# First expert group tile by tile, gather indices written from PSUM, and layer 0's tokens kept in the scatter banks

## The chip, the cores and the metric

One core of one Trainium2 chip. The metric is device time in microseconds (us) of one execution; a run's figure is a median over executions.

## The reference

Four layers work on x, 4 sequences of 256 tokens with 256 channels (1024 tokens in all). Each layer l first makes a gated input and then adds the result of a feed-forward part:

```
c = sigmoid(x) * ratio_l          # ratio_l: a two-way decayed scan over time of exp(k) and exp(k)*v (numerator / denominator)
x = x + ffn_l(c)
```

- Layer 0: every sequence picks its 32 best tokens by a router (128 picked tokens); they go through attention (16 heads) and an MLP of width 1024; the result, times a gate per token, is added at the picked tokens. x also gets c itself.
- Layer 1: mixture of 64 experts. sigmoid(c @ gate) are the scores; 4 of 8 groups of experts and then 6 experts are picked per token; each expert has 48 places (slots) and runs silu(g) * u, width 96, then a down product; the slots' results, times weights, are added to their tokens. A shared expert of width 96 is added for every token.
- Layer 2: 8 experts given as low-rank corrections of one shared MLP of width 704. Layer 3: a dense gated MLP of width 1024.

## The kernel before, in words

Each engine has one instruction list, written out by hand; engines wait for each other by semaphores. Channels lie on the partitions: `xT`, `cT` and so on are 128 partitions x 2 halves (`ct`) x 1024 tokens, and a product over all tokens is cut into two chunks (`ch`) of 512. So the eight PSUM banks of 512 columns hold, for instance, the four (`ct`, `ch`) pieces of a full result in banks 0 to 3. The scans of the ratios of later layers (`forth`, L742: forward scans; `back_again`, L753: backward scans; `den`, L759; `num_own`, L764; `num`, L769; `newton`, L776 and L778; `quotient`, L783) are spread by hand between VectorE's other work.

**End of layer 0.** TensorE sums the output projection `wo` (L1478), then runs filler products that nothing reads (`idle`, L1355), turns the normalized rows `xn` (L1425), runs the gate and up products (L1490) into banks 0 to 3 and the down product (L1495) into bank 5. VectorE adds `ao` and multiplies by the gate (L963, L964) to make `dl`; TensorE scatters `dl` by the one-hot matrix into banks 0 to 3 (L1500). VectorE had added `cT` to `xT` before (L959), and now adds each bank to `xT` (L970); ScalarE takes the sigmoid of `xT` (L477); VectorE multiplies by `ratio` (L792) to make the new `cT`, then runs four scans (L742).

**Routing of layer 1.** TensorE makes the logits (L1509), turns tokens to rows (L1362) and scores to rows (L1515); from there VectorE finds groups, experts and slots (L977 to L1032). Three 4-byte products (L1549) turn the slot numbers so that VectorE can write the token of each slot, first as numbers (`tokf`, L1035) and then cast to whole numbers (`toki`, L1037). The tokens' rows lie in DRAM (`token_rows`: 256 channels and 64 weights), written by SyncE's queue: rows at L316, weights `w1` at L318. GpSimd waits for these writes, clears two pads (L380) and issues indirect gathers (L391), three of 128 slots for each of 8 groups of 8 experts; the gathers of group g+2 wait until group g's hidden rows are turned. SyncE loads the weights of the next but one group (L307, L308) when a group's down product is done.

**The loop over 8 groups.** For each: `rows_in` turns the gathered rows (TensorE L1566, copies by ScalarE L589), `gate_up` (L1603), silu (L596), product (L1083), `turn_hidden` (L1612, copied at L604), `down` (L1629), scaled copies (L638, L639), the rest part (L1069), the one-hot matrices (L1063), and 24 scatter products into banks 0 to 3 (L1574), which run one group late. `slot_weights` is L1054 and L1055. VectorE's scans for layers 2 and 3 fill the rest. In group 0 the order of VectorE is: wait for all three gathers, `back_again(2, 0, 0)`, `forth(2, 0, 1)`, the products of the group, `slot_weights(0)`, `back_again(2, 0, 1)`, two `den`, one-hots, rests. On TensorE filler products stand before and after `rows_in(0)`, and two of the four products of the shared expert's down part (L1555) stand before it, two just before `down(0)`.

Of the kernel before, what the change touches and what calls it, by code (L numbers as in the profile page):

```python
# [24 lines left out]
P = 128  # L25
# [23 lines left out]
GE = 8  # L49
# [44 lines left out]
def build(nc, I, out):  # L94
    ctx = ExitStack()
    with ctx:
# [28 lines left out]
        rows1 = sb("rows1", [P, RRING, 2, C], F32R)  # L125
        bank = [ctx.enter_context(nc.psum_tensor(f"bank{i}", [P, CHUNK], F32)) for i in range(6)]
# [67 lines left out]
        spreadv = at(o + N, GE, CAP)  # L194
# [66 lines left out]

        def tail2(it):

            return it % H2T == H2T - 1
# [8 lines left out]
        def _(sp):  # L273
# [24 lines left out]
            sp.wait_ge(S("x1_ready"), 4)  # L298
# [52 lines left out]
        def _(pool):  # L351
# [23 lines left out]
            pool.wait_ge(S("x1_ready"), 4)  # L375
# [9 lines left out]
            for t in range(ST):  # L385
                if t % GT == 0 and t >= 2 * GT:
                    pool.wait_ge(S("h1_turned"), 2 * (t // GT - 1))
                if t >= XRING:
                    pool.wait_ge(S("xgT_done"), (t - XRING) // GT + 1)
                    pool.wait_ge(S("wslot_ready"), (t - XRING) // GT + 1)  # L390
                g.indirect_dma_start(xg[:, t % XRING, :], None, scratch[:, :],  # L391
                                     bass.IndirectOffsetOnAxis(ap=toki[:, t:t + 1].bitcast(U32), axis=0)
                                     ).then_inc(S(f"gather{t // GT % 4}"), 16)
# [22 lines left out]
        def _(act):  # L416
# [54 lines left out]
            def gate(l):  # L471
                for ct in range(CT):
                    if l == 0:
                        act.wait_ge(S("x_in"), 16)
                    else:
                        act.wait_ge(S(f"x{l}_ready"), 2 * ct + 2)
                    s.activation(cT[:, ct, :], xT[:, ct, :], ACT.Sigmoid).then_inc(S("sig_ready"), 1)  # L477

# [31 lines left out]
            gate(0)  # L510
# [50 lines left out]
            for j in range(2):  # L561
                act.wait_ge(S("gate0_done"), j + 1)
                s.activation(su0[:, 4 * j:4 * j + 4, :], bank[j][:].rearrange("p (a c) -> p a c", a=4), ACT.Silu).then_inc(S("silu0"), 1)

            gate(1)
# [18 lines left out]
            def rows_in(g):  # L584
                for ct in range(CT):
                    act.wait_ge(S("xgT_done"), g + 1)
# [19 lines left out]

            euk(2)
            rows_in(0)
# [98 lines left out]
        def _(dve):  # L707
# [80 lines left out]
            def cond(l):  # L788
                dve.wait_ge(S("ratio_ready"), l)
                for ct in range(CT):  # L790
                    dve.wait_ge(S("sig_ready"), 2 * l + ct + 1)
                    v.tensor_tensor(cT[:, ct, :], cT[:, ct, :], ratio[l % 2][:, ct, :], ALU.mult).then_inc(S("c_ready"), 1)  # L792
# [144 lines left out]
            num(1, 0)  # L937
            num(1, 1)
# [3 lines left out]
            v.tensor_copy(ao, bank[4][:, 0:C])  # L942
# [9 lines left out]
            for j in range(2):  # L952
# [3 lines left out]
                                bank[2 + j][:].rearrange("p (a c) -> p a c", a=4), ALU.mult).then_inc(S("hm0_ready"), 1)  # L956
                if j == 0:
                    for ct in range(CT):
# [988 lines left out]
```

## Time and profile before

| | |
|---|---|
| median of 3 runs | 456.92 us (455.61 to 457.77) |
| the profiled execution, its own time | 456.5 us |
| its span, first to last instruction | 454.7 us |
| granted TensorE clock, mean | 0.968 |
| busy: TensorE / VectorE / ScalarE / GpSimd | 88% / 79% / 47% / 24% |

Times in the profile count from the span's start. A busy share says nothing by itself of what sets the end; for that one follows which wait ends last in each stretch. A 4-byte float product appears as two instructions, one of type fp32r as one.

### The profile page before, as it was taken

The numbers are of one execution on the slowest core, as the hardware profiler recorded it, in microseconds if no ns is written. First come the engines' busy times: TensorE is split into PE (matmuls) and PEld (weight loads), VectorE is DVE, ScalarE is ACT, GpSimd is POOL, SyncE is SP. The second block draws the span as 40 slices with busy tenths as digits, with TensorE's granted clock in tenths as the row PEclk, the third lists the DMA queues.
The fourth block names the chain that finished last, engine by engine and source line by source line (L and its number), as shares of the span: only waits on it lengthen the run. The fifth ranks groups of instructions, "written<-read, shape, count | busy, mean of one in ns | idle before, by whom it ended". The sixth has DMA issues, their size and how long they took to land.

```text
span 454.7 us, 5110 instructions
## 1 busy us (share of the span) xinstructions
PE 400.9 (88%) x1680; PEld 216.3 (48%) x1680; DVE 360.4 (79%) x663; ACT 215.9 (47%) x398; POOL 108.5 (24%) x76
## 2 busy tenths in 40 slices
PE   0988999989988597998999999999999999998673
PEld 0433454677834255675677773444444344433220
DVE  4999969885989679897997879617986966449995
ACT  2864655563236645656774683521111141157780
POOL 1000004200000233343220000047684844540000
PEclk9999899989999599999999999999999999999897
DMA  7930000550039328775677530350000000000011
GB/s 278 396 155 1 2 0 0 210 196 0 1 129 322 104 64 222 209 237 159 214 232 241 215 116 1 138 233 0 1 0 0 0 0 1 1 0 0 1 48 46
DMA packets 12251, 47.45 MB, mean 104 GB/s; under 512 B 2897, under 2 KB 5434, under 8 KB 9794
## 3 DMA queue, kind: packets, MB, share of 16 engines
q1 hardware_dynamic: 11074, 43.20, 27.0%
q0 software_dynamic: 1152, 3.93, 3.8%
q8 instruction: 14, 0.23, 0.2%
q14 instruction: 11, 0.09, 0.1%
HBM read 44.76 MB, written 2.37 MB: 104 GB/s over the span
## 4 chain that ended last, share of the span: by engine, by line
PE 45%; DVE 29%; issue 14%; POOL 5%; DMA 4%; ACT 2%; POOLq 0%; DVEq 0%; SPq 0%
PE bank L1710 7%; PE bank L1697 6%; POOL arena L391 5%; PE bank L1574 4%; PE bank L1742 3%; PE bank L1739 3%; PE bank L1446 3%; DMA arena<-token_rows,arena 2%; PE bank L1355 2%; PE bank L1665 2%; PE bank L1490 2%; PE bank L1478 2%; PE bank L1629 1%; DMA vecs<-in_vecs 1%; DVE ekT L1319 1%
## 5 line engine op out<-in xcount | busy, mean ns | idle before, releaser
L676 ACT ACTIVATE early<-bank 128x512 f32<-128x512 f32 (+1 forms) x24 | 14.3, 597 | 86.0 <-PE bank L1710 76.6
L1574 PE MATMUL bank<-onehot,rows 128*128 128x512 f32 x192 | 52.4, 413 | 0.0
L1244 DVE TENSOR_TENSOR early<-early,bank 128x512 f32<-128x512 f32 (+1 forms) x24 | 16.4, 685 | 37.8 <-ACT early L676 34.3
L391 POOL DMA_INDIRECT arena<-token_rows,arena x24 | 30.6, 1275 | 54.4 <-PE bank L1612 48.5
L1710 PE MATMUL bank<-arena 128*128 128x512 f32 (+1 forms) x96 | 42.2, 600 | 0.1
L1574 PEld LDWEIGHTS bank<-onehot,rows 128*128 128x128 f32 x192 | 34.7, 193 | 10.3 <-issue 3.5
L1697 PE MATMUL bank<-cT,arena 128*128 128x512 f32 x80 | 37.9, 596 | 0.0
L402 POOL TENSOR_TENSOR early<-early,arena 128x512 f32<-128x512 f32 (+1 forms) x12 | 20.1, 1672 | 62.4 <-DMA arena<-pair_weights 55.6
L408 POOL TENSOR_TENSOR early<-early,arena 128x512 f32<-128x512 f32 x10 | 22.3, 2232 | 29.6 <-DVE early L1244 29.6
L1063 DVE TENSOR_SCALAR onehot<-const,arena 128x1024 fp32r<-128x1024 f32 x24 | 18.0, 754 | 10.7 <-PE bank L1574 10.3
L1710 PEld LDWEIGHTS bank<-arena 128*128 128x128 f32 (+1 forms) x96 | 15.7, 181 | 22.6 <-issue 21.2
L1697 PEld LDWEIGHTS bank<-cT,arena 128*128 128x128 f32 x80 | 14.9, 190 | 18.1 <-issue 18.1
L371 POOL TENSOR_TENSOR arena<-arena 128x512 f32<-128x512 f32 x6 | 8.0, 1335 | 63.9 <-DVE arena L908 63.9
L1742 PE MATMUL bank<-early,arena 128*128 128x512 f32 x48 | 22.8, 596 | 0.0
L1603 PE MATMUL bank<-arena 128*64 128x192 f32 x256 | 22.5, 329 | 0.1
L1629 PE MATMUL bank<-arena 96*64 96x256 f32 x192 | 22.5, 383 | 0.0
L1355 PE MATMUL bank<-const 128*128 128x512 f32 x42 | 22.0, 649 | 0.0
L1739 PE MATMUL bank<-early,arena 128*128 128x512 f32 (+1 forms) x48 | 21.3, 605 | 0.8 <-POOL early L406 0.8
L1762 PE MATMUL bank<-wkv_a,arena 128*128 128x512 bf16 x64 | 17.2, 409 | 5.1 <-DVE wkv_a L1217 2.6
L412 POOL TENSOR_TENSOR early<-early 128x512 f32<-128x512 f32 x10 | 21.0, 2100 | 1.6 <-PE bank L1742 0.9
L1603 PEld LDWEIGHTS bank<-arena 128*64 128x64 f32 x256 | 18.1, 137 | 5.0 <-issue 3.0
L1629 PEld LDWEIGHTS bank<-arena 96*64 96x64 f32 x192 | 13.1, 137 | 9.4 <-issue 3.6
(367 smaller groups left out, 858.9 us busy)
## 6 DMA issues: line engine op xcount, KB each, us to landing
arena<-in_w_gateup SPq DMA_DIRECT2D x16, 768.0 KB
arena<-in_w_down SPq DMA_DIRECT2D x8, 768.0 KB
arena<-in_wq SPq DMA_DIRECT2D x1, 2048.0 KB
arena<-in_wo SPq DMA_DIRECT2D x1, 2048.0 KB, 7.7
const<-in_const SPq DMA_DIRECT2D x1, 1688.0 KB, 10.7
arena<-in_w_upgate SPq DMA_DIRECT2D x1, 1408.0 KB, 5.8
kT<-in_kT SPq DMA_DIRECT2D x2, 512.0 KB, 4.9
xT<-in_xT SPq DMA_DIRECT2D x1, 1024.0 KB, 7.9
```

The lines of the kernel that those rows point to most:

```text
L391: g.indirect_dma_start(xg[:, t % XRING, :], None, scratch[:, :], bass.IndirectOffsetOnAxis(ap=toki[:, t:t + 1].bitcast(U32), axis=0)).then ...
L402: g.tensor_tensor(c1[r1], t1[r1], c1b[r1, cc], ALU.mult).then_inc(S("ch_ready"), 1)
L408: g.tensor_tensor(c2[r2], t2[r2], c2b[r2, cc], ALU.mult).then_inc(S("ch_ready"), 1)
L412: g.tensor_tensor(mix[r1], c1[r1], c2[r1], ALU.add).then_inc(S("ch_ready"), 1)
L1355: mm(bank[bk][:], ident, iota[:, 0:CHUNK], start=True, stop=True)
L1574: return mm(bank[2 * ct + ch][:], rows1[:, i % RRING, part, ct * P:(ct + 1) * P], onehot1[:, t, ch * CHUNK:(ch + 1) * CHUNK], start=False, ...
L1603: last = mm(bank[4 + p // 2][HALF * h:HALF * (h + 1), (p % 2) * 2 * F1:(p % 2 + 1) * 2 * F1], xgT[g % 2][:, ct, e * CAP:e * CAP + HALF], r ...
L1629: last = mm(bank[6 + t // 2][HALF * h:HALF * (h + 1), (t % 2) * C:(t % 2 + 1) * C], h1[:, RUN4 * j + lo:RUN4 * j + lo + HALF], r["d"][:, 4 ...
L1697: mm(bank[2 * (it % 2) + z][:], wug2[:, ct, z * 5 * P + f * P:z * 5 * P + (f + 1) * P], cT[:, ct, ch * CHUNK:(ch + 1) * CHUNK], start=(ct ...
L1710: last = mm(dst, (bup, bga)[z][:, f * P:f * P + fw], ((zu1, zg1), (zud, zgd))[k][z][:, ch * CHUNK:(ch + 1) * CHUNK], start=False, stop=Tru ...
L1739: mm(bank[6 + k][:], adn[rows2(it, k), f, :], cc_[rows2(it, k)], start=(f == 0), stop=(f == H2T - 1))
L1742: last = mm(bank[4 + ct][:], wdn2[:, f, ct * P:(ct + 1) * P], c1 if tail2(it) else mix, start=(f == 0), stop=False)
```

## The change

Two stretches are edited: from the `wo` product to the routing of layer 1, and from the slot numbers to the end of group 0.

```
# layer 0
VectorE:  xT += cT moves from between the two hidden products to before num(1, 1)   (L959)
          ao = wo result * gate (was a plain copy); dl = down * gate + ao in one instruction (was two)
          the four additions of the banks to xT are gone
TensorE:  idle(7, 5)  ->  keep_tokens(0), keep_tokens(1);   idle(7, 1)  ->  keep_tokens(2)
          gate and up products to banks 4 to 7, down product to bank 4, then keep_tokens(3)
          scatter products start=True -> start=False;  idle(6, 2) gone
+            def keep_tokens(i):
+                ct, ch = divmod(i, 2)
+                pe.wait_ge(S("c0_ready"), B + ct + 1)
+                mm(bank[i][:], ident, xT[:, ct, ch * CHUNK:(ch + 1) * CHUNK], start=True, stop=False)
ScalarE:
+            def gate1():
+                for i in range(4):
+                    ct, ch = divmod(i, 2)
+                    act.wait_ge(S("scatter0_done"), i + 1)
+                    s.activation(cT[:, ct, ch * CHUNK:(ch + 1) * CHUNK], bank[i][:], ACT.Sigmoid).then_inc(S("sig_ready"), 1)
+            def rows1_kept():        # four copies of banks 0 to 3 to xT, ahead of the scores' sigmoid
+                    s.copy(xT[:, ct, ch * CHUNK:(ch + 1) * CHUNK], bank[i][:]).then_inc(S("x1_ready"), 1)
VectorE:  the product with ratio in four pieces of 512 (was two of 1024); logits wait for each piece
SyncE and GpSimd no longer wait for x1_ready before the expert weights and the clears
TensorE waits for x1_ready only before it turns tokens to rows

# layer 1, slots
+        groups1 = sb("groups1", [P, GE], F32R)
+        spreadv = sb("spread1", [P, GE, CAP], F32R)          # L1549 becomes three one-pass products
+            v.tensor_copy(groups1[:], ofgroup)
+            v.tensor_scalar(toki.bitcast(U32).rearrange("p (g t) -> p t g", t=GT), slots,
+                            float(N), float(N), ALU.add, ALU.min).then_inc(S("toki_ready"), 1)
+            v.tensor_scalar(tokf.rearrange("p (g t) -> p t g", t=GT), slots, float(N), float(N), ALU.add, ALU.min).then_inc(S("toki_ready"), 1)

# layer 1, group 0
+        FIRST_GATHER = "gather0", "gather3", "gather2"       # one semaphore for each of the three gathers
+            def first_rows(t):                               # TensorE; ScalarE has one copy for each to match
+                pe.wait_ge(S(FIRST_GATHER[t]), 16)
+                for ct in range(CT):
+                    last = tr(bank[(6, 7, 0)[t]][:, ct * P:(ct + 1) * P], xg[:, t, ct * P:(ct + 1) * P], ident)
+                last.then_inc(S("xgT_done"), 1)
-            idle(6, 3)
-            rows_in(0)
-            idle(5, 1)
+            first_rows(0)
+            first_rows(1)
+            gate_up(0, (0,))
+            first_rows(2)
+            gate_up(0, (1, 2, 3))
+            shared_down(0, 0)
+            shared_down(0, 1)
ScalarE:  a Silu on one column after euk(2), before the first copies
VectorE:  forth(2, 0, 1) moves from right behind back_again(2, 0, 0) to behind slot_weights(0)
```

## Rows read from the trace of the kernel before

**Rows 1.** The page, busy time by engine.
```profile
PE 400.9 (88%) x1680; PEld 216.3 (48%) x1680; DVE 360.4 (79%) x663; ACT 215.9 (47%) x398; POOL 108.5 (24%) x76
```
**Rows 2.** Windows: stretch, length, busy us (instructions) by engine, clock, DMA share, GB/s.
```profile
162.00:175.00 13.00, 12.58 (x106) 8.81 (x106) 12.69 (x23) 9.26 (x23) 5.75 (x4) 1.00 0.32 74
187.00:199.00 12.00, 12.00 (x89) 8.78 (x88) 10.44 (x17) 7.35 (x15) 3.53 (x2) 1.00 0.84 225
```
**Rows 3.** Timeline, before the gate and up products: start, us, engine, line [idle before].
```profile
109.77 4.46 PE L1355 MATMUL bank<-const 128*128 128x512 f32 x10
109.97 0.42 DVE L940 TENSOR_TENSOR arena<-bank,arena 128x256 f32<-128x256 f32 x1 [3.08 <-PE bank L1478]
...
111.42 0.35 DVE L945 TENSOR_SCALAR arena<-arena 128x256 f32<-128x256 f32 x1
114.06 0.38 PE L1425 MATMUL bank<-const,arena 128*128 128x128 f32 x2
...
115.14 3.06 PE L1490 MATMUL bank<-arena 128*128 128x128 f32 x25
```
**Rows 4.** Timeline, from the hidden products of layer 0 to its scatter.
```profile
120.38 2.35 DVE L959 TENSOR_TENSOR xT<-xT,cT 128x1024 f32<-128x1024 f32 x2
...
122.39 3.62 PE L1495 MATMUL bank<-arena 128*128 128x256 f32 x16
...
126.11 0.42 DVE L963 TENSOR_TENSOR arena<-bank,arena 128x256 f32<-128x256 f32 x1
...
126.98 3.70 PE L1500 MATMUL bank<-arena 128*128 128x512 f32 x8 [0.97 <-DVE arena L964]
...
128.15 0.69 DVE L970 TENSOR_TENSOR xT<-xT,bank 128x512 f32<-128x512 f32 x1 [1.22 <-PE bank L1500]
```
**Rows 5.** The chain of waits, into the routing: start, us, what.
```profile
131.32 2.43 DVE cT L792 x2
...
136.38 0.70 DVE arena L977
```
**Rows 6.** Timeline, ScalarE's copies of four banks.
```profile
138.62 2.01 ACT L571 COPY arena<-bank 128x512 f32<-128x512 f32 x4
```
**Rows 7.** Timeline, from the slot numbers to group 0.
```profile
153.50 1.45 PE L1549 MATMUL bank<-const,arena 128*128 128x8 f32 x6 [5.68 <-DVE arena L1032]
...
154.78 0.20 POOL L380 MEMSET arena<- 128x32 f32 x2 [22.25 <-DMA token_rows<-arena]
...
155.21 0.18 DVE L1037 CAST arena<-arena 128x24 uint32<-128x24 f32 x1
...
161.67 2.68 DVE L753 TENSOR_TENSOR_SCAN wkv_c<-dec,ends,wkv_c 128x256 f32<-128x256 f32 x4 [5.09 <-DMA arena<-token_rows,arena]
...
164.21 2.82 PE L1603 MATMUL bank<-arena 128*64 128x192 f32 x32
...
166.91 0.35 DVE L1083 TENSOR_TENSOR arena<-arena,bank 128x192 f32<-128x192 f32 x1
```
**Rows 8.** The chain of waits, the first gathers.
```profile
155.68 1.16 POOL arena L391
...
158.40 3.24 DMA arena<-token_rows,arena
```
**Rows 9.** Timeline, TensorE's first work of group 1 after its wait.
```profile
178.86 0.42 PE L1612 MATMUL bank<-const,arena 128*96 128x128 f32 x2 [2.52 <-DVE arena L1083]
```
**Rows 10.** Windows with the clock at half (columns as in Rows 2).
```profile
150.00:159.00 9.00, 5.50 (x11) 2.95 (x12) 4.89 (x14) 5.49 (x11) 2.91 (x5) 0.50 0.25 55
180.00:183.00 3.00, 3.00 (x10) 2.06 (x8) 3.00 (x5) 2.20 (x4) 1.12 (x1) 0.50 1.04 264
```
**Rows 11.** Timeline, a gather that landed late (group 4).
```profile
198.59 0.80 SPq L307 DMA_DIRECT2D arena<-in_w_gateup  x2
...
199.41 0.95 POOL L391 DMA_INDIRECT arena<-token_rows,arena  x1 [0.30 <-issue]
...
208.15 0.87 PE L1566 MATMUL bank<-const,arena 128*128 128x128 f32 x6 [2.12 <-DMA arena<-token_rows,arena]
```

More of the change, by code:

```diff
@@ L509, in _ @@
             euk(0)
-            gate(0)
+            gate0()
             for j in range(4):
@@ L562, in _ @@
                 act.wait_ge(S("gate0_done"), j + 1)
-                s.activation(su0[:, 4 * j:4 * j + 4, :], bank[j][:].rearrange("p (a c) -> p a c", a=4), ACT.Silu).then_inc(S("silu0"), 1)
-            gate(1)
+                s.activation(su0[:, 4 * j:4 * j + 4, :], bank[(4, 6)[j]][:].rearrange("p (a c) -> p a c", a=4), ACT.Silu).then_inc(S("silu0"), 1)
+            gate1()
+            rows1_kept()
             act.wait_ge(S("logit1_done"), 1)
@@ L605, in hidden_copy @@
                        bank[4 + j][0:F1, 0:4 * HALF].rearrange("f (e c) -> f e c", c=HALF)[:, :, 0:CAP]).then_inc(S("h1_ready"), 1)
+            def first_rows(t):
+                act.wait_ge(S("xgT_done"), t + 1)
+                s.copy(xgT[0][:, :, t * P:(t + 1) * P],
+                       bank[(6, 7, 0)[t]][:, 0:C].rearrange("p (a c) -> p a c", a=CT)).then_inc(S("xgT_ready"), 1)
             euk(2)
-            rows_in(0)
+            s.activation(ws1[:, 0:1], ws1[:, 0:1], ACT.Silu)
+            for t in range(GT):
+                first_rows(t)
             for g in range(NG):
@@ L1046, in _, with all_gathered @@
             shared_product(1)
[L1047 removed]
+            def all_gathered(g):
+                if g:
+                    dve.wait_ge(S(f"gather{g % 4}"), gathered(g))
+                else:
+                    for name in FIRST_GATHER:
+                        dve.wait_ge(S(name), 16)
+            all_gathered(0)
             back_again(2, 0, 0)
[L1049 removed]
             def slot_weights(g):
[L1052 removed]
+                all_gathered(g)
                 i = g * GT
@@ L1494, in _ @@
                 pe.wait_ge(S("hm0_ready"), f // 4 + 1)
-                last = mm(bank[5][:, 0:C], hm0[:, f, :], wd0[:, f, :], start=(f == 0), stop=(f == F0T - 1))
+                last = mm(bank[4][:, 0:C], hm0[:, f, :], wd0[:, f, :], start=(f == 0), stop=(f == F0T - 1))
             last.then_inc(S("down0_done"), 1)
+            keep_tokens(3)
             pe.wait_ge(S("dl_ready"), 1)
@@ L1548, in _ @@
             for t in range(GT):
-                last = mm(bank[4][:, t * NG:(t + 1) * NG], spreadv.rearrange("e g c -> e (g c)")[:, t * P:(t + 1) * P], ofgroup,
+                last = mm(bank[4][:, t * NG:(t + 1) * NG], spreadv[:].rearrange("e g c -> e (g c)")[:, t * P:(t + 1) * P], groups1[:],
                           start=True, stop=True)
```

112 lines of the change are left out of this document (50 added, 62 removed).

## The prediction

> **What bounds the kernel now.** I read the page first, for the shares: TensorE is busy 88% of the span and VectorE 79% [rows 1], so neither share alone says what sets the end, and the stretches have to be read one by one. Then the windows: in the stretch of group 0 VectorE is busy 12.69 of 13.00 us, and from group 2 on TensorE is busy 12.00 of 12.00 [rows 2]. The chain of waits and the timeline fill in the rest, and in them I look only at the two stretches that the change edits, because all that stands before and after is untouched and can only be shifted. The reader should see four facts. (1) Ahead of the gate and up products TensorE is not waiting for data: `xn` is written at 111.42 + 0.35 = 111.77, but TensorE turns it only at 114.06, because ten filler instructions hold it for 4.46 us from 109.77 [rows 3]. (2) From the scatter to the routing the path is a relay: scatter, addition, sigmoid, product with the ratio, four scans, and routing at 136.38 [rows 4, 5]. (3) From there to the slot numbers VectorE runs alone and TensorE idles, for 5.68 us before the slot products [rows 7]. (4) VectorE waits 5.09 us for the three first gathers, and from their landing at 158.40 + 3.24 = 161.64 it works almost without a gap until TensorE, which has been idle for 2.52 us, is let go at 178.86 [rows 7, 8, 9]. After that TensorE is the bound. So a gain counts if it brings the landing of the gathers forward, or shortens VectorE's work from there to 178.86.
>
> **The change part by part.** Times are those of the trace before, and each shift is counted against it.
>
> *Fillers ahead of the MLP.* Ten filler instructions cost 4.46 us, 0.446 each. Two `keep_tokens` are four such instructions, 1.78 us: from 109.77 to 111.55. Then `xn` (111.77) is late next, and the turning starts at about 111.82 instead of 114.06: gain 2.24 us [rows 3]. `keep_tokens(2)` is as long as the filler that it replaces. The additions of `cT` to `xT` (2.35 us, [rows 4]) move into VectorE's wait of 3.08 us for the `wo` product [rows 3]; they are hidden with 0.7 us to spare, and without that cover the whole 2.35 would stand ahead of `xn`. `ao` with a scalar costs what the copy did, and lies beside ScalarE's square root.
>
> *The MLP and its end.* Gate and up, and the down product (3.62 us, [rows 4]), only change banks. VectorE loses the additions between the two hidden products, but these ended at 120.38 + 2.35 = 122.73 and the up products only just before the down products began at 122.39, so the second hidden product was at most 0.3 us late, and the down products had their first half to do meanwhile: 0. `dl` by one instruction of about 0.42 instead of two (126.11 to 126.98, 0.87) saves 0.45 us on VectorE. But `keep_tokens(3)`, two instructions of 0.446, stands on TensorE between down product and scatter: it ends 0.89 us after the down product, while `dl` is there 0.09 + 0.43 = 0.52 after it. So the scatter starts 0.89 us behind the down product instead of 0.96 (126.98 against 126.02, the product's end). Gain 0.07; sum 2.3.
>
> *From scatter to routing.* Before: the first bank is read at 128.15, the last when the scatter ends, 126.98 + 3.70 = 130.7, and the last `cT` stands at 131.32 + 2.43 = 133.75, 3.05 us after the last bank [rows 4, 5]. After: sigmoid of 512 columns from PSUM, which I take at ScalarE's copy of the same shape (four in 2.01, so 0.50 in a row, [rows 6]) plus 0.1 for one alone, then a product of 512 columns on VectorE at 0.69 as L970 has it, and a hand-over: 0.6 + 0.05 + 0.7 = 1.35 after the last bank. Gain 1.7. Bounds: 1.2 if all pieces queue, 2.0 if less. The path then forks. VectorE goes on with four scans. TensorE must end the logits, ScalarE must end `rows1_kept`, four copies, 2.01 us [rows 6], before the scores' sigmoid, which is queued behind them. The copies end 0.6 + 2.0 = 2.6 us after the last bank, the logits about 1.35 + 0.9 for two product instructions + 0.2 of hand-overs = 2.45: the copies decide by 0.15, and take back 0.1 to 0.3 of the gain. Behind the waiting sigmoid stand the scaling for a scan and the row copies, all with time to spare. Gain so far 2.3 + 1.7 - 0.2 = 3.8, and the routing starts at 136.38 - 3.8 = 132.6.
>
> *Slots.* VectorE's search in between is untouched; the small copy to `groups1` adds at most what the small cast L1037 takes, 0.18 [rows 7], in a place where VectorE waits for TensorE's counts; I take 0. Six product instructions in 1.45 us become three: 0.24 each, 0.72 [rows 7]; gain 0.7 (no less than 0.4, no more than 0.9). `toki` straight from PSUM saves the cast, 0.18 and its hand-over: 0.2 [rows 7]. That would be 0.9, but GpSimd also waits for the write of `w1`, and this write only moves with the routing (3.8). It releases the clears at 154.78 and they end at 154.98, against a first gather at 155.68 [rows 7, 8]. The write and the clears are late next: 154.98 - 3.8 + 0.3 for the issue = 151.4, so the first gather gains 4.3 us, 0.5 from this part and not 0.9. Expert weights start with the scatter's end (124.7 + 3.7 = 128.4) and no longer wait for the last addition (130.7 + 0.7): 3 us earlier, out of the way of the `w1` write as before.
>
> *Group 0.* The last gather lands at 161.64 - 4.3 = 157.3. TensorE before needs 164.21 + 2.82 - 161.64 = 5.4 us from there to the end of gate and up [rows 7, 8]; by tiles, with one quarter done, it needs two turnings (0.4), then three quarters of 2.82, 2.5 us in all. That is 2.9 us more for TensorE, but VectorE does not use it: its list from landing to TensorE's release holds the same work in another order, `back_again` 2.68 first, after which both silu are ready within 0.1 us (157.3 + 2.5 + some 0.4 for the silu, against 157.3 + 2.7 + 0.35 for the first product). Before, VectorE had idled only a few tenths there (its product stands at 166.91, right behind the scans). So I count 0 for this edit (at most 0.2), and TensorE, 7 us early with `down(0)`, waits for VectorE in group 1 for longer than 2.52 us. The two `shared_down` in between lie in that slack. `tokf` after `toki` costs 0.2 in VectorE's wait for the gathers.
>
> Sum: 2.3 + 1.7 - 0.2 + 0.5 + 0 = 4.3 us. The profiled execution took 456.5, so 452.2; the median of the runs shown is 0.4 above that execution, so 452.6.
>
> **The clock.** TensorE runs at half clock (0.50) from 150 to 159 and again from 180 to 183 [rows 10], each time after an idle stretch, of 5.68 and 2.52 us [rows 7, 9]. The change leaves the first idle stretch as it is, removes the fillers that came before and after `rows_in(0)`, and lengthens the second. If the clock is not back when the last gather lands, gate and up of three quarters take 2.1 us longer, VectorE's second product is late by about that, and a longer low clock in group 1 costs some tenths: a loss of 2.1. The Trainium skill, "TensorE: Matmul & The Clock Gate", section "Why this matters for your kernels", speaks for this rival: it advises not to leave gaps between bursts of products, and the change takes out products that filled such a gap. By that rule the time is 454.7, by the rows' sum 452.6; the trace agrees with the rule in that both half-clock stretches follow an idle one.
>
> **Rivals.**
> - *Half clock at group 0.* 452.6 + 2.1 = 454.7. For it: rows 10. Against it: TensorE still has two filler instructions and four `shared_down` ones, some 5 us at half clock, before the first gather lands. Chance 0.20.
> - *The gathers start with the index list.* If the `w1` write lands sooner, or VectorE finds a tenth here and there, the gain is 4.7 to 5.5: 451.7. Chance 0.10.
> - *No change.* The gain at the front is real but is taken back later: VectorE's and TensorE's loop is aligned with loads, and a longer low-clock stretch in group 1 (the present one, 180 to 183, cost half of 3 us) or `rows1_kept` ahead of the scores' sigmoid eats it. 456.5. Chance 0.13.
> - *Slower: gathers behind the weights.* In group 4 the last gather was issued at 199.41, after the group's weights at 198.59, and TensorE waited 2.12 us for it [rows 11]. It decides as soon as a group's last gather is issued after the weights of the same phase. If the shifted order makes four more groups wait so, 4 x 2.12 = 8.5 against 4.3: 452.6 + 8.5 = 461.1. Against it: the order inside groups 1 to 7 is unchanged, and both queues shift together. Only group 2's gathers move against their weights. Chance 0.07.
>
> **How the numbers follow.** My forecast has 0.50, the rivals 0.20, 0.10, 0.13 and 0.07. A measurement of this kernel tells 0.5% (2.3 us) from no change, so faster means below 454.6. Faster: 0.50 + 0.10 + half of the clock's rival, 0.10, and a little of the fourth, 0.02 = 0.72. Same: 0.21. Slower: 0.07. The range reaches from 5.9 us of gain (all upper bounds: 2.3 + 2.0 + 0.9 + 0.2, and half a us of the clock) to the clock's rival with 0.7 more: 451.0 to 455.4; it holds the first three cases, 0.80.
>
> **What would show it.** TensorE's turning of `xn` right after `xn` is written, near 111.8; scatter start near 124.7; the four sigmoids 0.86 apart; the first routing instruction (L977 before) near 132.6; three slot products of 0.2 to 0.3 us; first gather near 151.4, released by the `w1` write and not by `toki`; last landing near 157.3; end of gate and up 2.5 us later; TensorE let go in group 1 near 174.5 after a wait for VectorE. The prediction is wrong if VectorE has gaps in group 0, if the clock is low after 157, or if the groups from 2 on take longer than before.

## The result, and the profile after

The changed kernel takes 452.85 us (median of 5, 451.23 to 454.70) against 455.90 for the kernel before on the same chip: a ratio of 0.9927 [0.9898, 0.9957], 3.1 us less. In 12 more executions, beside 35 of the kernel before at 456.01, it took 452.53 (450.18 to 454.53), ratio 0.9930 [0.9898, 0.9961], 3.5 us less. (Executions more than 1.5% above the fastest of their kernel are left out of the ratios, not of the medians.) The forecast was 452.6, 4.3 us less than the median of 456.92 that stood for the kernel before. The kernel before now has a median 1.0 us lower, and the fall is about 1 us smaller than forecast; the two cancel. That the median stands so near 452.6 is luck, and the fall of 3.1 to 3.5 us is what the working has to answer for.

The execution whose profile is read here is the longest of the first five, 454.7. That is the very time of the clock's rival, and the profile shows that the clock had a part in it. A second profile of the same kernel, from an execution of 453.1, is read beside it. Places in traces are best compared from VectorE's `x1` on (109.97 in [rows 3]), the addition behind the `wo` product, because the place of `x1` itself differs by almost 4 us between the executions (108.60 to 112.44). It is 109.49 after, and 111.10 in the second profile. "From `x1`" below means this difference. From the loop's end to the last instruction it takes 181.2 to 181.6 us in all 14 profiles, so `x1` and the loop's end account for the whole time.

The mark has one weakness. TensorE's list up to the `wo` product is untouched, but VectorE's two additions of `cT` to `xT` now stand ahead of `x1`. In the two profiles of the change `x1` starts 0.20 us behind the end of the `wo` product, as before. In four of the experiments it does not; the table below says which.

The page after: span, TensorE's, VectorE's and ScalarE's busy time, and the clock in 40 slices.

```profile
span 452.8 us, 5081 instructions
...
PE 399.1 (88%) x1661; PEld 215.3 (48%) x1661; DVE 357.8 (79%) x661; ACT 217.8 (48%) x406; POOL 106.8 (24%) x76
...
PEclk9999899989999587999999999999999999999798
```

Against [rows 1] the sums hardly move: 1.8 us less on TensorE, 2.6 on VectorE. They say nothing of where 3 us went, so the stretches are read one by one. First the timeline after, from the additions of `x1` to the routing (start, us, engine, line, tile, idle time before and its releaser).

```profile
109.29 1.88 PE L1508 MATMUL bank<-xT,const 128*128 128x512 f32 x4
109.49 0.42 DVE L965 TENSOR_TENSOR arena<-bank,arena 128x256 f32<-128x256 f32 x1 [0.81 <-PE bank L1502]
...
111.35 0.44 PE L1449 MATMUL bank<-const,arena 128*128 128x128 f32 x2 [0.18 <-DVE arena L971]
...
112.49 7.41 PE L1521 MATMUL bank<-arena 128*128 128x128 f32 x64
...
124.06 3.60 PE L1532 MATMUL bank<-arena 128*128 128x512 f32 x8
...
127.69 0.60 ACT L485 ACTIVATE cT<-bank 128x512 f32<-128x512 f32 x1 [0.26 <-PE bank L1532]
...
128.18 2.05 ACT L490 COPY xT<-bank 128x512 f32<-128x512 f32 x4
128.32 0.69 DVE L815 TENSOR_TENSOR cT<-cT,ratio 128x512 f32<-128x512 f32 x1 [0.17 <-ACT cT L485]
...
130.18 0.60 ACT L581 ACTIVATE arena<-bank 128x512 f32<-128x512 f32 x1
...
131.62 0.69 DVE L992 TENSOR_TENSOR arena<-bank,early 128x512 f32<-128x512 f32 x1
```

The reader is to see three things. The turning of `xn` (L1449) now follows VectorE by 0.18 us; four `keep_tokens` instructions take the place of ten fillers. The scatter starts 14.57 us from `x1`, before 17.01: a gain of 2.44. The last `cT` stands at 129.01, 19.52 from `x1` against 23.78, so the tail behind the scatter gave another 1.82. The routing starts 22.13 from `x1` against 26.41 [rows 5]: 4.28 earlier, and 22.12 in the second profile.

Now the timeline after, from the slot numbers to the end of group 0, which answers to [rows 7] and [rows 8].

```profile
148.74 0.80 PE L1580 MATMUL bank<-groups,spread 128*128 128x8 f32 x3 [5.68 <-DVE spread L1048]
...
149.57 0.19 DVE L1052 TENSOR_SCALAR arena<-bank 128x24 uint32<-128x24 f32 x1 [0.90 <-PE bank L1580]
...
150.01 0.20 POOL L385 MEMSET arena<- 128x32 f32 x2 [21.31 <-DMA token_rows<-arena]
...
150.84 1.16 POOL L396 DMA_INDIRECT arena<-token_rows,arena  x1 [0.63 <-issue]
...
156.33 1.55 PE L1642 MATMUL bank<-arena 128*64 128x192 f32 x8
...
157.18 2.68 DVE L774 TENSOR_TENSOR_SCAN wkv_c<-dec,ends,wkv_c 128x256 f32<-128x256 f32 x4 [6.14 <-DMA arena<-token_rows,arena]
...
158.43 3.98 PE L1642 MATMUL bank<-arena 128*64 128x192 f32 x24
...
160.39 0.35 DVE L1106 TENSOR_TENSOR arena<-arena,bank 128x192 f32<-128x192 f32 x1 [0.53 <-ACT arena L610]
...
162.83 0.35 DVE L1106 TENSOR_TENSOR arena<-arena,bank 128x192 f32<-128x192 f32 x1 [2.08 <-ACT arena L610]
...
176.79 0.66 PE L1651 MATMUL bank<-const,arena 128*96 128x128 f32 x2 [2.81 <-DVE arena L1106]
```

The first gather stands 41.35 from `x1` against 45.71: 4.36 earlier. VectorE takes up its scans at the landing, 47.69 against 51.70: 4.0 earlier. But then it waits 0.53 and 2.08 us for the two silu, because three quarters of gate and up take 3.98 us. The same stretch in the second profile of this kernel:

```profile
158.78 2.68 DVE L774 TENSOR_TENSOR_SCAN wkv_c<-dec,ends,wkv_c 128x256 f32<-128x256 f32 x4 [6.15 <-DMA arena<-token_rows,arena]
...
159.13 2.17 PE L1642 MATMUL bank<-arena 128*64 128x192 f32 x24
...
161.37 0.69 DVE L1106 TENSOR_TENSOR arena<-arena,bank 128x192 f32<-128x192 f32 x2
```

Here the three quarters take 2.17 us and both products stand in a row with no wait. The windows tell what differs (length, busy us and instructions by engine, granted clock, DMA share, GB/s), first in the profile after, then in the second.

```profile
154.00:159.00 5.00, 4.56 (x20) 2.25 (x20) 1.82 (x3) 1.12 (x3) 3.77 (x4) 0.50 0.54 126
159.00:163.00 4.00, 4.00 (x26) 2.60 (x23) 1.39 (x4) 0.66 (x2) 0.00 (x0) 0.61 0.16 44
```

```profile
154.00:159.00 5.00, 4.13 (x17) 1.65 (x16) 0.22 (x1) 0.74 (x2) 3.78 (x5) 0.76 0.49 122
159.00:163.00 4.00, 4.00 (x30) 2.44 (x29) 3.92 (x9) 1.03 (x3) 1.29 (x1) 1.00 0.36 93
```

The clock is at half (0.50) from 145.1 to 162.2 in the one and from 146.1 to 156.4 in the other, with the same instructions in the same order. One execution gets 2.4 GHz back before the products need it, the other only as they end.

The gain can be followed through the whole program in one table: us from `x1` to VectorE's scans at the landing, to the first one-hot of group 0, to TensorE's gate and up of group 2, and to the first product of layer 2 behind the last scatter (L1665 before, L1705 after), where the loop is over.

| | landing | one-hot, group 0 | gate and up, group 2 | loop over |
|---|---|---|---|---|
| before | 51.70 | 63.35 | 79.88 | 163.31 |
| after, first profile | 47.69 | 61.90 | 79.59 | 161.96 |
| after, second profile | 47.68 | 59.17 | 76.18 | 158.68 |

In the second profile the 4.0 us of the landing are 3.7 at group 2 and 4.6 at the end. In the first, 2.6 go in group 0 and another 1.2 in group 1, so that 0.3 are left at group 2 and 1.3 at the end. From group 2 on both profiles are about 1 us shorter than the one of before (82.4 and 82.5 against 83.4), in groups that the change doesn't touch; whether that comes with the change isn't shown. The first profile's 454.7 is 1.8 us below the 456.5 of before: 1.3 from this table, and 0.5 from the untouched part ahead of `x1`. So the gain at the front is in both executions, and most of what comes through is decided between 157 and 180 us.

### The profile page after: what moved, and what is told of

Same layout as the page of the kernel before. It is cut to its first block, busy times and chain, and to the rows that moved or that the text cites. A ratio compares the mean times of both kernels' runs of the same rounds, so it can differ in the third digit from the quotient of the medians.

```text
span 452.8 us, 5081 instructions
## 1 busy us (share of the span) xinstructions
PE 399.1 (88%) x1661; PEld 215.3 (48%) x1661; DVE 357.8 (79%) x661; ACT 217.8 (48%) x406; POOL 106.8 (24%) x76
## 4 chain that ended last, share of the span: by engine, by line
PE 46%; DVE 27%; issue 15%; POOL 4%; DMA 4%; ACT 3%; POOLq 0%; DVEq 0%; SPq 0%
PE bank L1750 7%; PE bank L1737 6%; POOL arena L396 4%; PE bank L1603 4%; PE bank L1782 3%; PE bank L1779 3%; PE bank L1470 3%; DMA arena<-token_rows,arena 2%; PE bank L1642 2%; PE bank L1705 2%; PE bank L1521 2%; PE bank L1502 2%; PE bank L1668 1%; DVE ekT L1343 1%; DVE ekT L1346 1%
## 5 line engine op out<-in xcount | busy, mean ns | idle before, releaser
L396 POOL DMA_INDIRECT arena<-token_rows,arena x24 | 29.2, 1216 | 59.4 <-PE bank L1651 53.5
L1642 PE MATMUL bank<-arena 128*64 128x192 f32 x256 | 25.2, 353 | 0.0
L774 DVE TENSOR_TENSOR_SCAN wkv_c<-dec,ends,wkv_c 128x256 f32<-128x256 f32 x16 | 10.7, 731 | 6.2 <-DMA arena<-token_rows,arena 6.1
```

What stands on the lines that cost most here:

```text
L1642: last = mm(bank[4 + p // 2][HALF * h:HALF * (h + 1), (p % 2) * 2 * F1:(p % 2 + 1) * 2 * F1], xgT[g % 2][:, ct, e * CAP:e * CAP + HALF], r ...
```

## The experiments

Each kernel ran 12 times beside the kernel before on the same chip (the last two 6 times), with one profile. Three chips were used: one for again, layer0_only, group0_only and fed_search, one for scans_first to early_pads, one for the last four. Nothing of the computation is left out in any. Ratios are to the kernel before on the same chip, with their 95% intervals, and kernels of different chips are compared by them.

One table for their profiles, in the columns above, with the stretch of half clock ahead of or in group 0 (us in that profile, and its end from `x1`; before it ends at 159.4 or 49.4, after at 162.2 or 52.7, in the second profile at 156.4 or 45.3):

| | median us, ratio | landing | one-hot | group 2 | loop over | half clock, end from `x1` |
|---|---|---|---|---|---|---|
| layer0_only | 455.62, 0.9964 [0.9930, 0.9999] | 48.27 | 60.92 | 78.33 | 162.21 | 144.8 to 158.5, 48.4 |
| group0_only | 456.85, 1.0021 [0.9992, 1.0049] | 51.76 | 63.37 | 79.62 | 163.31 | 149.8 to 160.1, 48.6 |
| fed_search | 456.27, 0.9992 [0.9957, 1.0027] | 47.48 | 61.69 | 78.84 | 163.33 | 152.3 to 162.6, 52.1 |
| scans_first | 453.88, 0.9938 [0.9893, 0.9983] | 47.46 | 58.86 | 76.30 | 158.96 | 146.9 to 157.1, 45.2 |
| fed_all | 453.38, 0.9947 [0.9912, 0.9982] | 47.47 | 58.96 | 75.22 | 161.31 | 142.2 to 145.6, 37.0 |
| fillers_back | 456.99, 1.0013 [0.9980, 1.0047] | 47.47 | 61.65 | 78.93 | 162.90 | 147.4 to 157.7, 45.5 |
| early_pads | 452.40, 0.9939 [0.9902, 0.9975] | 47.44 | 58.93 | 75.88 | 159.08 | 144.5 to 154.7, 44.9 |
| layer0_no_fill | 455.94, 0.9988 [0.9950, 1.0026] | 47.40 | 60.42 | 76.63 | 159.05 | 146.2 to 163.2, 52.7 |
| before_no_fill | 457.17, 1.0004 [0.9970, 1.0039] | 51.68 | 65.50 | 80.12 | 165.01 | 150.8 to 161.1, 48.6 |
| gathers_first | 449.12, 0.9850 [0.9797, 0.9902] | 47.46 | 59.08 | 75.90 | 155.49 | 146.9 to 157.2, 45.3 |
| both_mends | 450.31, 0.9885 [0.9836, 0.9935] | 47.48 | 59.02 | 75.84 | 155.43 | 146.3 to 156.5, 45.3 |

In layer0_only, fed_all, early_pads and layer0_no_fill `x1` starts 0.93 or 0.94 us behind the end of the `wo` product (TensorE's next instruction marks it), and not 0.20 as in all others. VectorE has no wait there, as in early_pads:

```profile
108.67 1.22 DVE L790 TENSOR_TENSOR wkv_a<-wkv_a,wkv_d 128x1024 f32<-128x1024 f32 x1
108.87 1.88 PE L1508 MATMUL bank<-xT,const 128*128 128x512 f32 x4
...
109.81 0.42 DVE L965 TENSOR_TENSOR arena<-bank,arena 128x256 f32<-128x256 f32 x1
```

So 0.7 us of the front's gain are lost ahead of `x1` in these four, where the columns don't show them: 0.7 belongs on each of their entries when they are compared with other rows. They are also just the four profiles without a stretch of half clock between 97 and 103 us; the other ten have one of 3.4 us there (98.0 to 101.4 before). Without it the `wo` product ends sooner against VectorE's list: 5.85 us behind the start of `num_own` in early_pads (103.02 to 108.87), 7.49 in the first profile of the change (101.80 to 109.29). Then the moved additions are no longer covered.

**again**: the changed kernel, unedited, for a second profile and a better median.

> The changed kernel itself, once more. Its profiled execution took 454.7 us, but others took 451.23 and 451.6. Theory A (the clock): executions differ in when TensorE's clock comes back after the search for slots. In the profiled one it was back at 162, after the last gather's landing at 157.2, and VectorE waited 0.53 + 2.08 us for gate and up; an execution in which it is back before the landing should take 451 to 452, with no such waits, and one in which it is not 453 to 455. Theory B (the order): the waits come from the new order alone, since VectorE no longer has four scans to run while gate and up are made; then a profile with an earlier clock still shows about 2 us of waits.

Its profile is read above. It is theory A's picture, the clock back at 156.4, ahead of the landing, and no wait of VectorE for gate and up. It took 453.1 and not 451 to 452, with an `x1` 1.6 us later than in the first profile.

**layer0_only and group0_only**: the change cut in two. The first has layer 0's edits, with group 0 and the slots as before; the second the reverse.

```
layer0_only = before + keep_tokens, gate1, rows1_kept, ao and dl, the four pieces
group0_only = before + one-pass slot products, toki from PSUM, first_rows, order of group 0
```

> Only the edits to layer 0 (tokens kept in the scatter banks, sigmoid from the banks, fused dl, logits by pieces); slots and group 0 as before. By the prediction's sum 2.3 + 1.7 - 0.2 = 3.8 us faster than the kernel before, so 452.1 against 455.9. If the sum of the whole is right but the two halves are not what I think, this would gain under 2.5 us. The fillers of group 0 are in place here, so by theory A its executions should spread less than those of the whole change.

> Only the edits to slots and group 0 (one-pass slot products, indices from PSUM, rows by tiles, scans behind slot_weights); layer 0 as before. By the prediction's sum 0.5 us faster (the first gather is held by the write of the weights w1), so 455.4. Theory A: in executions whose clock is late it loses up to 2.1 and is 1.6 slower than before, so 455.4 to 457.5. Theory B: always about 1.5 slower.

By their ratios layer 0's edits alone bring 1.6 us (the interval reaches to nearly nothing), less than half of the 3.8 expected; the others alone bring nothing, and together they bring 3.2. The parts don't seem to add up, but the intervals of layer0_only and of the change overlap, so this isn't shown. The column "landing" shows that the slots give nothing (51.76 against 51.70), and that in layer0_only the landing is 3.4 us earlier from `x1`, 2.7 from the end of the `wo` product. Nor did its executions spread less, as expected: 450.35 to 456.3, against 450.18 to 454.53. The timeline of layer0_only around the landing shows a part of what is lost behind it.

```profile
156.40 3.79 PE L1356 MATMUL bank<-const 128*128 128x512 f32 x6
...
158.34 2.68 DVE L760 TENSOR_TENSOR_SCAN wkv_c<-dec,ends,wkv_c 128x256 f32<-128x256 f32 x4 [5.57 <-DMA arena<-token_rows,arena]
160.02 0.82 PE L1574 MATMUL bank<-const,arena 128*128 128x128 f32 x6
...
165.06 0.35 DVE L1084 TENSOR_TENSOR arena<-arena,bank 128x192 f32<-128x192 f32 x1 [0.88 <-ACT arena L603]
```

Six fillers still hold TensorE when the tokens have landed: they end 1.7 us after the landing, two more follow, and VectorE waits 0.28 and 0.88 us. In the kernel before the same six ended only 0.7 us after the landing (the tokens are turned from 162.39, the scans start at 161.67), and VectorE had no wait for the silu [rows 7].

**fed_search**: the changed kernel with fillers in TensorE's idle stretch of 5.68 us, to keep the clock up (the clock's theory).

```
             last.then_inc(S("counts1_done"), 1)
+            idle(4, 5)
             pe.wait_ge(S("spreadv_ready"), 1)
```

> The changed kernel with five filler products on TensorE (bank 4, 4.5 us) in the stretch in which VectorE searches for the slots and TensorE idled for 5.68 us. Theory A: the clock never falls there, slot products, shared products and gate and up run at full clock in every execution; VectorE has no wait over 0.5 us for gate and up; the median is that of the fastest executions or better, 450.3 to 451.3, with less spread. Theory B: no change against the changed kernel, 452.9.

It did what it was to do in the search and nothing behind it, and the median is that of the kernel before. Its timeline has the fillers and three slot products at full clock, and then gate and up of group 0 almost as slow as in the first profile.

```profile
144.00 4.56 PE L1379 MATMUL bank<-const 128*128 128x512 f32 x10
149.75 0.50 PE L1581 MATMUL bank<-groups,spread 128*128 128x8 f32 x3 [1.19 <-DVE spread L1048]
...
159.60 3.62 PE L1643 MATMUL bank<-arena 128*64 128x192 f32 x24
```

The slot products take 0.50 instead of 0.80 at full clock, and then the clock falls all the same, at 152.3, during the shared expert's products, and returns only at 162.6. The Trainium skill, "TensorE: Matmul & The Clock Gate", section "Why this matters for your kernels", advises to leave no long gaps between bursts of products. By it this should have helped, and the trace doesn't agree: filling the longest gap moved the half-clock stretch later without removing it. TensorE had waited 1.19 and 0.59 us and was busy 1.97 of the 3.70 us before the clock fell (148.6 to 152.3).

**scans_first**: the change with VectorE's scans in the order of before, to see whether the scans behind the gathers matter.

```
             back_again(2, 0, 0)
+            forth(2, 0, 1)
...
                 if g == 0:
-                    forth(2, 0, 1)
                     back_again(2, 0, 1)
```

> The changed kernel with the four scans of forth(2, 0, 1) back in their old place, before group 0's products. Theory B (cover): the scans hid up to 2.5 us of gate and up when the clock was low at the landing; in such an execution VectorE's two waits (0.53 and 2.08 us in the first profile of the changed kernel) shrink to under 0.3, so the slow executions become 2 us faster and the median falls by about 1, to 451.5 against 452.5. If the losses come from TensorE's clock elsewhere (group 1) or from late gathers, the median doesn't move by more than 0.5.

The ratio is 0.9938 against 0.9930 for the change, 0.4 us apart, and the two intervals overlap widely: the order alone shows no effect. Its profile (one-hot at 58.86) is as good as the second one of the change. Whether it matters in executions whose clock comes back late isn't settled.

**fed_all**: fillers in the search, more behind the slots, and one group ahead of each of the first two turnings.

```
+            idle(4, 5)                 # behind the counts products
...
-            idle(6, 1)
+            idle(6, 3)
             shared_down(1, 0); shared_down(1, 1)
+            idle(6, 1)
             first_rows(0)
+            idle(5, 1)
             first_rows(1)
```

> The changed kernel with filler products on TensorE from the counts to the last landing: five in the search, two more behind the slot products, one before the first tile and one before the second. With the five in the search alone the clock still fell, at 152.9, right after the slot products. Theory A: with no idle stretch left up to the landing the clock stays full, gate and up end 2.5 us after the landing, first product of VectorE right behind the scans; all executions lie at or below 452, the median at 451. Theory C: TensorE's clock before the landing is not what splits the executions; then the median stays at 452.5 to 456, as with the fillers in the search alone (456.3).

**fillers_back**: the change with the fillers that stood around `rows_in(0)`.

```
+            idle(6, 3)
             first_rows(0); first_rows(1)
+            idle(5, 1)
             gate_up(0, (0,))
```

> The changed kernel with only the removed fillers of group 0 back: three before the first tile and one before its gate and up. If their removal is what keeps the clock low past the landing, it now returns by about 159 as before the change, and the median gains 0.5 to 1 (452.0 or less). If the stretch of half clock is set by the idle search alone, the fillers run at half clock (0.89 each instruction instead of 0.45), hold the first tile until about 160 and make it 1 to 2 us slower: 454.

Both have fillers ahead of the tiles; they differ in the clock. In fed_all it is whole from 145.6 on, through all of group 0, and no filler holds anything:

```profile
151.13 1.88 PE L1587 MATMUL bank<-arena,early 96*128 96x512 f32 x4
...
153.93 1.02 PE L1379 MATMUL bank<-const 128*128 128x512 f32 x2
...
158.67 0.69 DVE L1106 TENSOR_TENSOR arena<-arena,bank 128x192 f32<-128x192 f32 x2
```

The last filler ends at 154.95, the landing is at 156.07, and VectorE's two products stand in a row. Group 2 starts 75.22 from `x1` (75.9 with the 0.7 of above), as early as in gathers_first. But from there its loop takes 86.09 us instead of some 82.5, with TensorE waiting 4.0 us for gathers, and the median is 453.4, no better than without. In fillers_back the clock is back at 157.7, ahead of the landing as in the second profile of the change, and still group 0 is slow. Its timeline says why.

```profile
153.94 3.63 PE L1586 MATMUL bank<-arena,early 96*128 96x512 f32 x4
...
157.36 2.91 PE L1379 MATMUL bank<-const 128*128 128x512 f32 x6
...
159.63 2.68 DVE L774 TENSOR_TENSOR_SCAN wkv_c<-dec,ends,wkv_c 128x256 f32<-128x256 f32 x4 [5.90 <-DMA arena<-token_rows,arena]
...
160.10 0.60 PE L1624 MATMUL bank<-const,arena 128*128 128x128 f32 x4
...
163.95 0.35 DVE L1106 TENSOR_TENSOR arena<-arena,bank 128x192 f32<-128x192 f32 x1 [1.63 <-ACT arena L610]
```

The six fillers end after the landing, so the first tile is turned after all three have landed, and VectorE waits 1.63 and then 0.94 us. Of the landing's 4.2 us only 1.7 are left at the one-hot, and the median, 456.99, lies above both of the expected values. The clock has its part in it all the same: the two fillers behind the slots and the four shared products ahead of the six ran at half clock, 2.05 and 3.63 us where fed_all has them at full clock in about 1.0 and 1.88. By these rows, as an estimate, the six would have ended 2.8 us sooner at full clock, ahead of the landing. So it takes both, the fillers and the half clock in front of them.

**early_pads**: the clears no longer wait for the write of `w1`, only the gathers do.

```
-            pool.wait_ge(S("rows_out"), 48)      # ahead of the clears
+            pool.wait_ge(S("rows_out"), 32)
...
-            pool.wait_ge(S("rows_out"), 48)      # ahead of the first gather
+            pool.wait_ge(S("x_in"), 32)          # on which the w1 write now counts
```

> The changed kernel with GpSimd's two small clears no longer waiting for the write of the weights w1 (they wait for the row write alone); the gathers still wait for w1. In the profile of the changed kernel w1 was down at 150.01, the clears followed, and the first gather began 0.83 us later, at 150.84, while the index list had been there at 149.76. If this hand-over holds the gathers, the first one now begins about 0.3 us after w1 is down, 0.5 us earlier, and the median gains 0.5 (452.0); if the index list or GpSimd's start-up of a gather holds it, nothing moves.

From the slot products to the first gather it takes 2.10 us in this profile (149.05 to 151.15), as in the one after (148.74 to 150.84), with the clears out of the way. So the clears held nothing. The chain of waits shows the write of `w1` as the last to arrive, first after, then early_pads:

```profile
147.40 2.57 DMA token_rows<-arena
```

```profile
147.72 2.57 DMA token_rows<-arena
...
150.33 0.82 issue
151.15 1.16 POOL arena L396
```

The write is down at 149.97 and at 150.29, 0.2 us behind the index list (149.76 and 150.08), and the gather begins 0.87 and 0.86 us after it, with the clears in between or without. In the kernel before the index list came last, and the gather began 0.28 us after it (155.40 to 155.68).

**layer0_no_fill and before_no_fill**: layer0_only, and the kernel before, each without the fillers around `rows_in(0)`.

```
             shared_down(1, 1)
-            idle(6, 3)
             rows_in(0)
-            idle(5, 1)
```

> Layer 0's edits alone, with the fillers around rows_in(0) taken out as well, but no tiles, no new order, old slot products. So far layer 0 alone gained 0.4 to 1.6 us of its 4.3 (455.6), the whole change 3.4, and the whole change with the fillers of group 0 put back 0.3 (457.0 against 457.3). Theory D (coupling): the fillers run at half clock up to the landing that layer 0 brings forward, and hold TensorE; taking them out lets the gain through. Then this kernel gains 3 or more, like the whole change, and the tiles are worth under 1 us. If the tiles are what lets it through, this one stays within 1 us of layer 0 alone.

> The kernel before with only the fillers around rows_in(0) taken out. There the turning of the rows began 0.75 us after the landing, and gate and up one filler later. Theory D: up to 0.75 us faster when the clock is back in time, up to 1.5 slower when it is not; so the median moves by less than 1, and the fillers matter only together with layer 0's edits. If the fillers cost by themselves, it gains 2 or more.

Neither gains at the median: 455.94 and 457.17. By the ratios the change is 2.6 us faster than layer0_no_fill, with intervals that just overlap. So the change's group 0 seems to be more than its missing fillers: behind layer 0's edits the turning and products by tiles are likely needed as well. No run parts them from the slot edits and the early Silu. The profile of layer0_no_fill is of an execution of 452.90, well below its median, and can't carry the column's 159.05 for the kernel; in its median the gain isn't there. In both profiles the 32 gate and up instructions of group 0 run in one block after the landing, mostly at half clock, in 4.13 us and in 5.22, against 2.82 in [rows 7]. That fits with the medians, but it is one profile of each.

**gathers_first and both_mends**: the change, with a group's weight loads held until the gathers of that group have landed; the second also has early_pads' edit.

```
             def experts(g):
                 if g >= 2:
                     sp.wait_ge(S("ffn1_done"), g - 1)
+                    sp.wait_ge(S(f"gather{g % 4}"), gathered(g))
```

> The changed kernel, with SyncE's weight loads of group g held until the gathers of group g have landed. In all profiles so far the rows of group 4 were late: gate and up of group 4 began 14.8 to 16.6 us after those of group 3 where a full group takes 12.5, and group 7's were late by 0.3 to 1.9. Theory E (late gathers, the prediction's fourth rival): the weights in front of the gather in the DMA queues cost that; holding them takes 2 us and more off the loop, and the median falls to 450.5. The weights come 3 to 4 us later, and have some 4 to spare. If the gather is late because GpSimd makes its descriptors slowly, or the weights are now late, nothing is gained.

> The changed kernel with both mends: weights held until the gathers have landed, and GpSimd's clears freed from the write of w1. If they add up, 0.2 to 0.5 below the run with the first alone: 450.1.

The fourth rival's mechanism, a gather behind the weights, stands in the profile after as it did in [rows 11]: weights at 197.82, the last gather at 198.64, TensorE let go at 207.41.

```profile
197.82 0.80 SPq L313 DMA_DIRECT2D arena<-in_w_gateup  x2
...
198.64 0.95 POOL L396 DMA_INDIRECT arena<-token_rows,arena  x1 [0.30 <-issue]
...
207.41 0.88 PE L1595 MATMUL bank<-const,arena 128*128 128x128 f32 x6 [2.15 <-DMA arena<-token_rows,arena]
```

In gathers_first the last gather is issued at 197.29 and the weights at 200.21, and TensorE turns the rows at 203.75 with no wait.

```profile
197.29 0.95 POOL L397 DMA_INDIRECT arena<-token_rows,arena  x1 [0.30 <-issue]
...
200.21 0.80 SPq L314 DMA_DIRECT2D arena<-in_w_gateup  x2
...
203.75 0.82 PE L1596 MATMUL bank<-const,arena 128*128 128x128 f32 x6
```

The windows from 200 to 212, first after, then gathers_first (columns as before):

```profile
200.00:212.00 12.00, 9.85 (x78) 7.09 (x78) 11.54 (x24) 5.40 (x10) 2.21 (x2) 1.00 0.66 212
```

```profile
200.00:212.00 12.00, 12.00 (x90) 8.87 (x89) 11.54 (x23) 7.78 (x15) 3.06 (x3) 1.00 0.76 239
```

TensorE has no gap left, and every group of the loop follows the last by 12.48 us (gate and up at 187.74, 200.22, 212.70, 225.18, 237.66); in the kernel before one of them took 14.8 (202.33 to 217.16). From gate and up of group 2 to the loop's end it is 79.59 us in both kernels, against 82.50 in the second profile of the change and 83.43 before: 2.9 us. The median is 449.12, where the change had 452.5 on another chip; by the ratios the two are 0.8% or 3.6 us apart. With 6 executions of each, gathers_first and both_mends can't be told apart (449.1 and 450.3).

## Why the prediction was right, and where it was not

**Front, 3.8 forecast: right, 4.28.** The fillers and `keep_tokens` gave 2.44 for 2.3, the tail behind the scatter 1.82 for 1.7. The 0.2 that `rows1_kept` was to take back did not come: the copies end at 130.23 and the logits at 130.14, so the sigmoid (130.18) waits for both together. One term held only in part: the additions were to be "hidden with 0.7 us to spare", a spare read from one execution, with the clock at half from 98.0 to 101.4. Without such a stretch they stick out by 0.7 us, in four of the eleven profiles with these edits.

**Slots, 0.5 forecast: mis-sized, 0.1.** From the slot products to the first gather it was 2.18 us and is 2.10. The products shortened as forecast, 1.45 to 0.80, and the first gather is released by the write of `w1`, as forecast. But "0.3 for the issue" was wrong: behind the write the gather begins 0.87 us after it is down, and early_pads shows the same without the clears. The 0.3 holds only where the index list comes last, as before. And group0_only shows that the slot edits alone move the landing by nothing (51.76 against 51.70). The gather gains 4.36 instead of 4.3, the front's surplus making up for the slots.

**Group 0, counted at 0: the step whose reason failed.** "VectorE does not use it" holds for the kernel before (group0_only: 1.0021), but not behind a front that is 4 us faster. Layer 0 alone brings 1.6 us and the whole change 3.2, by the ratios, so behind the faster front the tiles and the missing fillers are worth some 1.6 us. That difference isn't clear of the noise; the next one is. The working named the removed fillers only as a danger to the clock. fillers_back shows the other side: with them back the whole gain is gone (1.0013 against 0.9930, with intervals apart). An edit counted at nothing should have been checked against the shifted times, where the fillers end after the landing (160.02 and 158.34 in layer0_only).

**The clock, rival at 0.20: under-rated.** It is what happened in the execution profiled first: VectorE waited 2.6 us where 2.1 were priced, and by the forecast's own signs ("VectorE has gaps in group 0", "the clock is low after 157") it is wrong for this execution. That its time was the rival's 454.7 to the tenth is chance: group 1 cost 1.2 more and the loop gave 1.1 back. In the second profile it did not happen: gate and up end 2.5 us after the landing, and TensorE is let go in group 1 4.3 us earlier from `x1`, both as forecast. The forecast treated the clock as a property of the kernel; it is also one of the execution. The 35 executions of the kernel before that ran beside **again** point the same way without any change: the 24 with a mean granted clock of 0.965 or more took 455.1 us on average, the 11 others 457.4. It isn't the whole story, since the fastest execution of the changed kernel, 450.18, had 0.959. So "452.6 or 454.7" was no choice. On the medians of the kernel before beside which it was measured (455.90 and 456.01) the sum of 4.3 gives 451.6 to 451.7 and the rival 453.7 to 453.8, and the changed kernel lies between them (452.85 and 452.53).

**Group 1's half clock** grew as the third rival feared: 3.4 us of it before (179.9 to 183.3), 6.8 after (175.8 to 182.6), with TensorE's wait at 176.79 now 2.81 instead of 2.52 [rows 9] and another of 1.71 ahead of it. In the second profile it is 6.8 too (173.4 to 180.3). From the one-hot to group 2 it takes 1.2 us longer than before in the first profile and 0.5 in the second.

**Gathers behind the weights**: the slower rival did not come, since the queues shifted together, as argued. But the loss it names was there in the profile of the kernel before too, and was as large a prize as the change: 2.9 us from group 2 to the loop's end.

**Open**: why layer0_no_fill has no gain at its median, with a profile that has one; what the scans' order is worth; why layer 0's edits alone bring so much less than the landing gains; and what decides in which executions the clock returns late. Too few profiles at the slow end were taken for it.

## What to carry to other kernels

Follow a gain through to the end by a few marks common to all kernels, relative to the last untouched instruction: here some 4 us at the landing became anything from 0 (fed_search) to 4.6 at the loop's end, with the fillers, the clock and the late gathers in between. Such a mark must be untouched on its own engine too: `x1` hid 0.7 us. And a cover read from one execution may be missing in the next. When a shift brings data forward, check each filler and each block that was just in time before against the new time. And look for the neighbour of every rival: the wait of 2.1 us for a late gather, listed as a danger, was removed by holding the weights by one wait, and was worth as much as the whole change.

## What the runs showed of the hardware

- The granted clock stayed at half for 17.1 us (145.1 to 162.2) in one execution and 10.2 (146.1 to 156.4) in another of the same kernel, though TensorE was busy 4.56 of 5.00 us from 154 to 159 in the first and 4.13 in the second. More fillers moved it (152.3 to 162.6 in fed_search) or cut it to 3.4 us (fed_all), and neither made the median better.
- Three products of 128x8 with fp32r operands took 0.50 us at full clock and 0.80 at half; six of fp32 took 1.45 at half [rows 7].
- A gather issued 0.8 us after 2 weight loads landed 8.8 us later (198.64 to 207.41); issued ahead of them it had landed within 2.9 us, since the weights that wait for it went out at 200.21 (issue 197.29).
- The first indirect gather began 0.87 us after the DMA write that it waits for was down, with two clears in between (149.97 to 150.84), and 0.86 without them (150.29 to 151.15, early_pads); 0.28 us after the index list where that came last (155.40 to 155.68, before). From one gather to the next GpSimd has 0.30.
- In ten profiles the granted clock was at half for 3.4 us between 97 and 103 us (98.0 to 101.4 before), in four not, with the same instructions up to there.
